# A graph network kernel: x loaded in five pieces with its statistics ahead of the edge keys, and the weight bounds' column sums made by VectorE

## The reference

```
xn = layernorm(x)
gnn: three times  h = x @ W; agg = sum over edges of h[src] * dinv[src] * dinv[dst] + h * dinv^2 + b
     x = layernorm(relu(agg)) * g + beta           (widths 1024, 512, 256)
mix: z = logmap0(proj(xn));  h = z @ w_qkv;  batchnorm over the nodes, relu
     s = depthwise and grouped 1x1 of h;  linear attention of [h, s];  w_res;  projections onto the ball
x = x + gnn + mix
ffn: of layernorm(x) the rows with the 1561 greatest router weights go through gelu(x @ w1 + b1) @ w2 + b2
out = x + ffn's part
```

## Time and profile before

| what | value |
|---|---|
| three runs | 1561.70, 1556.98, 1564.74 us, median 1561.7 |
| the profiled execution | 1556.77 us, span 1554.9 us |
| TensorE busy | 1381.6 us, 89% of the span |
| VectorE, ScalarE, GpSimd busy | 56%, 35%, 35% |
| chain of waits, by engine | PE 67%, DVE 24%, issue 4%, DMA 2%, ACT 2%, POOL 1% |
| GpSimd's scatters | 416, 436.8 us busy and 127.9 between them, the first at 81.75 us |
| load of the flag into a register | three steps on VectorE's queue at L637, 16.8 to 17.7 us |

### The profile page before, as it was taken

One profiled execution on the slowest core, in us unless ns is written; L12 is line 12 of the kernel. 1 busy time (PEld: TensorE's weight loads), 2 busy tenths in 40 slices (PEclk: granted clock), 3 DMA queues, 4 the chain that ended last, 5 costly groups with the idle time before them and its releaser, 6 DMA issues.

```text
span 1554.9 us, 20788 instructions
## 1 busy us (share of the span) xinstructions
PE 1381.6 (89%) x7353; PEld 948.3 (61%) x7353; DVE 867.7 (56%) x1519; ACT 538.1 (35%) x952; POOL 545.6 (35%) x537
## 2 busy tenths in 40 slices
PE   0998997987973899999999999999999899958995
PEld 0576765655752566666666666666666555646775
DVE  6674167758669255555555322222222598778766
ACT  1315062423421344444444323222222122337962
POOL 1078777777777777500000000000000852023100
PEclk9997699998986999999999999999999999989998
DMA  9940000000022222221222032222222344310002
GB/s 292 299 145 1 1 1 1 1 1 1 1 57 55 67 61 59 71 69 51 68 70 60 21 115 61 61 60 60 60 60 60 101 121 133 89 41 1 1 1 83
DMA packets 46076, 99.53 MB, mean 64 GB/s; under 512 B 18962, under 2 KB 31135, under 8 KB 45885
## 3 DMA queue, kind: packets, MB, share of 16 engines
q1 hardware_dynamic: 32698, 98.55, 22.3%
q0 software_dynamic: 13312, 0.13, 0.6%
HBM read 75.79 MB, written 22.85 MB: 63 GB/s over the span
## 4 chain that ended last, share of the span: by engine, by line
PE 67%; DVE 24%; issue 4%; DMA 2%; ACT 2%; POOL 1%; DVEq 0%; SPq 0%; ACTq 0%; POOLq 0%
PE psum L1506 63%; DVE scr L877 5%; DVE scr L1100 4%; PE psum L1797 1%; DVE scr L1058 1%; DMA rows<-in_x 1%; POOL acc L529 1%; DVE scr L879 1%; DVE scr L1051 1%; DVE scr L875 1%; DVE big L1035 1%; DVE scr L1062 1%; DVE scr L1048 1%; DVE scr L1045 1%; DVE scr L882 1%
## 5 line engine op out<-in xcount | busy, mean ns | idle before, releaser
L508 POOL DMA_INDIRECT counts<-big,eidx x416 | 436.8, 1050 | 200.8 <-issue 127.9
L1506 PE MATMUL psum<-rows,scr 125*125 125x512 f16 x1250 | 278.3, 381 | 11.6 <-DVE scr L1048 9.4
L1506 PE MATMUL psum<-big,scr 125*125 125x512 f16 x1250 | 278.5, 379 | 1.0 <-DVE big L952 1.0
L1506 PEld LDWEIGHTS psum<-rows,scr 125*125 125x125 f16 x1250 | 170.2, 137 | 113.6 <-DVE scr L1048 10.1
L1506 PEld LDWEIGHTS psum<-big,scr 125*125 125x125 f16 x1250 | 169.7, 136 | 95.4 <-DVE big L952 1.5
L524 POOL MEMSET big<- 128x4 f16 x1 | 0.1, 115 | 557.0 <-PE psum L1506 557.0
L1506 PE MATMUL psum<-wb,scr 128*125 128x512 f16 x600 | 133.7, 379 | 0.0
L1506 PEld LDWEIGHTS psum<-wb,scr 128*125 128x125 f16 x600 | 81.7, 136 | 47.8 <-ACT scr L1358 0.3
L924 DVE TENSOR_SCALAR scr<-psum,col 125x256 f32<-125x256 f32 x25 | 12.1, 484 | 172.0 <-PE psum L1506 172.0
L1506 PE MATMUL psum<-wb,big 128*125 128x256 f16 x600 | 76.2, 281 | 23.7 <-DVE big L1111 21.1
L1506 PE MATMUL psum<-big,wm 128*128 128x313 f32 x312 | 91.3, 436 | 2.4 <-issue 2.4
(11 more groups left out here) (346 smaller groups left out, 2087.2 us busy)
## 6 DMA issues: line engine op xcount, KB each, us to landing
scr<-counts SPq DMA_DIRECT2D x75, 683.6 KB
counts<-wb SPq DMA_DIRECT2D x25, 683.6 KB
counts<-big,eidx POOLq DMA_INDIRECT x416
scr<-counts SPq DMA_DIRECT2D x75, 79.3 KB
scr<-in_x SPq DMA_DIRECT2D x25, 125.0 KB
rows<-in_x SPq DMA_DIRECT2D x1, 2800.0 KB
out<-acc SPq DMA_DIRECT2D x5, 560.0 KB
wb<-in_w SPq DMA_DIRECT2D x1, 2048.0 KB, 10.9
```

The source lines that it names most:

```text
L508: pool.indirect_dma_start(cells, bass.IndirectOffsetOnAxis(ap=eidx[:, r * EQ + g:r * EQ + g + 1], axis=0), evalue[:, at_c:at_c + 1], None, ...
L1506: return pe.matmul(o, l, r, start=start, stop=stop)
```

## The change

- x is loaded in five pieces of five tiles, each with its own semaphore, and the clears are issued only when the last has landed. VectorE takes the statistics of a piece when it is there.
- On VectorE the keys, the flag and its load into a register come behind z's scale.
- ScalarE loads the table of the square root before it waits for the variance.
- On TensorE the flag's sum, the Gram rows, the rounds, the turnings and the degree products are put in another order.
- The bounds: VectorE sums the columns of `ssw`, `ssg`, `ssb` and `ss1` into seven columns (`sums7`), and TensorE adds these over the partitions with one call in place of 40.

In the diff, the moved block of keys and flag is shown once, where it is added; `sums7` is seven new columns in `col`.

```diff
@@ -75,9 +75,9 @@
     "bounds_read", "n4root_done", "tanh_done", "fnorm_done",
 )
 DVE_MILESTONES = (
-    "flag_part", "flag_ready", "xvar_done", "ratio2_done", "ratio_done", "zscale_ready",
+    "xvar_done", "ratio2_done", "ratio_done", "zscale_ready", "flag_part", "flag_ready",
     "index_ready", "value_ready", "edges_ready", "reach_ready", "needed_ready", "needs_ready",
-    "nzrow_done", "gram_copied", "dinv_read", "wp_done", "bnvar_done", "bn_done", "be2w_read",
+    "nzrow_done", "gram_copied", "dinv_read", "squares_summed", "wp_done", "bnvar_done", "bn_done", "be2w_read",
     "n4_ready", "f4_ready", "fscale_done", "router_done", "negw_done", "least_done", "last_done",
     "bound_found",
 )
...
@@ -358,9 +359,12 @@
         dst_w = bass.AP(a["dst_pad"].tensor, PADE - HALO, [[EC, ER], [1, EW]])
         load(edst_i, dst_w, "edges_loaded")
         load(esrc_i, src_w, "edges_loaded")
-        load_rows(x_rows, a["x"].rearrange("(t p) d -> p t d", p=P), "x_loaded")
+        x_tiles = a["x"].rearrange("(t p) d -> p t d", p=P)
+        for c in range(NC):
+            load_rows(x_rows[:, c * G:(c + 1) * G, :], x_tiles[:, c * G:(c + 1) * G, :], f"x{c}_loaded")
 
         sp.wait_ge(sem("zi_ready"), 2)
+        sp.wait_ge(sem(f"x{NC - 1}_loaded"), ROWS_IN)
         for t in range(T):
             load_rows(counts_dram[t], zi[:, (T - 1 - t) * P:(T - 1 - t) * P + N], "counts_cleared")
         load(wq, a["wq"].rearrange("(k p) n -> p k n", p=128), "mixw_loaded")
@@ -613,31 +617,9 @@
             done.settle()
 
 
-        dve.wait_ge(sem("edges_loaded"), 32)
-        edge_keys(dve, done, ekey, esrc, edp, edt, wkey)
...
-        dve.wait_ge(sem("x_loaded"), ROWS_IN)
         for t in range(T):
+            if t % G == 0:
+                dve.wait_ge(sem(f"x{t // G}_loaded"), ROWS_IN)
             done.did(dve.bn_stats(stats[:, t, :], x_rows[:, t, :]))
         done.settle()
         for t in range(T):
@@ -690,6 +672,29 @@
         done.settle()
         dve.scalar_tensor_tensor(out=z_shift, in0=means, scalar=-1.0, in1=z_scale, op0=ALU.mult,
                                  op1=ALU.mult).then_inc(milestone("zscale_ready"), 1)
+
+        dve.wait_ge(sem("edges_loaded"), 32)
+        edge_keys(dve, done, ekey, esrc, edp, edt, wkey)
+        dstf = wkey
+        done.did(dve.tensor_copy(dstf, edst_i))
+        done.settle()
+        mid, nxt, far_ = (free(dstf, HALO + s, [[1, EC]]) for s in (0, 1, HALO))
+        done.did(dve.tensor_tensor(fwd, mid, nxt, ALU.is_gt))
+        done.did(dve.tensor_tensor(bwd, mid, far_, ALU.is_equal))
+        done.settle()
+        done.did(dve.scalar_tensor_tensor(out=bwd, in0=mid, scalar=float(N), in1=bwd, op0=ALU.is_lt, op1=ALU.mult))
+        done.settle()
+        done.did(dve.tensor_tensor(fwd, fwd, bwd, ALU.max))
+        done.settle()
+        dve.tensor_reduce(flagf[:ER], fwd, AX, ALU.max).then_inc(milestone("flag_part"), 1)
+        dve.wait_ge(sem("flag_sum"), 1)
+        done.did(dve.tensor_scalar(flagf[0:1], bank(7, 1, 1), 1.0, None, ALU.min))
+        done.settle()
+        dve.tensor_copy(flagi[0:1, 0:1], flagf[0:1]).then_inc(milestone("flag_ready"), 1)
+
+
+        dve.wait_ge(milestone("flag_ready"), AFTER["flag_ready"])
+        far = dve.value_load(flagi[0:1, 0:1], min_val=0, max_val=1)
 
         done.settle()
         for r in range(ROUNDS_EQ):
@@ -778,6 +783,11 @@
             done.did(dve.tensor_tensor(gw[:, k, 0:512], bank(4 + 2 * k, 128, 512), wq[:, k, 0:512], ALU.mult))
             last = dve.tensor_tensor(gw[:, k, 512:768], bank(5, 128, 256, 256 * k), wq[:, k, 512:768], ALU.mult)
             last.then_inc(sem("wgw_done"), 1)
+        dve.wait_ge(sem("squares_done"), 2)
+        for n, (part, lo, hi) in enumerate(((ssw, 0, 8), (ssg, 0, 8), (ssb, 0, 8), (ssw, 8, 12), (ssg, 8, 12),
+                                            (ssb, 8, 12), (ss1, 0, 4))):
+            last = dve.tensor_reduce(sums7[:, n:n + 1], part[:, lo:hi], AX, ALU.add)
+        last.then_inc(milestone("squares_summed"), 1)
         for m in range(NT):
             last = dve.tensor_scalar(wp[:, m, :], wp[:, m, :], wdw[:, m:m + 1], None, ALU.mult)
         last.then_inc(milestone("wp_done"), 1)
@@ -1195,6 +1205,7 @@
 
         act.wait_ge(sem("ident_ready"), 1)
         act.copy(ident16[:, :], ident[:, :]).then_inc(milestone("ident16_ready"), 1)
+        act.preload_act_table(ACT.Sqrt)
         act.wait_ge(sem("eps_ready"), 2)
         act.wait_ge(milestone("xvar_done"), AFTER["xvar_done"])
         act.activation(rstd, ca, ACT.Sqrt).then_inc(milestone("xroot_done"), 1)
@@ -1506,8 +1517,6 @@
             return pe.matmul(o, l, r, start=start, stop=stop)
 
         pe.wait_ge(sem("ident_ready"), 3)
-        pe.wait_ge(milestone("flag_part"), AFTER["flag_part"])
-        mm(bank(7, 1, 1), ones[:ER, 0:1], flagf[:ER], True, True).then_inc(sem("flag_sum"), 1)
 
         pe.wait_ge(milestone("ident16_ready"), AFTER["ident16_ready"])
 
@@ -1565,31 +1574,33 @@
             return last
 
         turn_z(0)
-        gram_rows(0, 2)
+        gram_rows(0, 3)
+        pe.wait_ge(milestone("flag_part"), AFTER["flag_part"])
+        mm(bank(7, 1, 1), ones[:ER, 0:1], flagf[:ER], True, True).then_inc(sem("flag_sum"), 1)
+        gram_rows(3, 6)
         count_alike(0)
+        gram_rows(6, 7)
         count_alike(1)
-        gram_rows(2, 4)
+        gram_rows(7, 8)
         count_alike(2)
-        gram_rows(4, 5)
+        turn_z(1)
         count_alike(3)
-        turn_z(1)
-        gram_rows(5, 10)
+        gram_rows(8, 12)
+        turn_z(2)
         turn_edges("index", 2, bwd)
         turn_edges("value", 3, fwd)
-        turn_z(2)
-        gram_rows(10, 11)
+        gram_rows(12, 13)
         turn_reach()
-        gram_rows(11, 12)
+        gram_rows(13, 14)
         turn_needed()
-        for b in range(T - 12):
-            last = gram_rows(12 + b, 13 + b)
-            if b < T - 13:
-                degree(b)
+        for b in range(T - 14):
+            degree(b)
+            last = gram_rows(14 + b, 15 + b)
             if b == 3 or b == 7:
                 turn_z(3 if b == 3 else 4)
         last.then_inc(sem("zsum_done"), 1)
-        degree(T - 13)
-        degree(T - 12)
+        for b in range(T - 14, EC // EB - 2):
+            degree(b)
 
         pe.wait_ge(milestone("nzrow_done"), AFTER["nzrow_done"])
         for m in range(2):
@@ -1597,7 +1608,7 @@
         for k in range(2):
             last = mm(bank(1, 128, 1, 416 + k), zrow[:, k * 128:(k + 1) * 128], ones[0:1, 0:1], True, True)
         last.then_inc(sem("gram_done"), 1)
-        for b in range(T - 11, EC // EB):
+        for b in range(EC // EB - 2, EC // EB):
             degree(b)
 
         pe.wait_ge(milestone("gram_copied"), AFTER["gram_copied"])
@@ -1626,16 +1637,8 @@
             last = mm(bank(5, P, D2), free(be1c[:, k:k + 1], 0, [[0, P]]), w2[:, k, :], k == 0, k == 7)
         last.then_inc(sem("be2w_done"), 1)
 
-        pe.wait_ge(sem("squares_done"), 2)
-        for k in range(4):
-            mm(bank(6, 128, 1, 22), ones[:, :], ss1[:, k:k + 1], k == 0, k == 3)
-        n = 0
-        for L, nk in ((0, 8), (1, 4)):
-            for s in (ssw, ssg, ssb):
-                for k in range(nk):
-                    last = mm(bank(6, 128, 1, 16 + n), ones[:, :], s[:, 8 * L + k:8 * L + k + 1], k == 0, k == nk - 1)
-                n += 1
-        last.then_inc(sem("bounds_done"), 1)
+        pe.wait_ge(milestone("squares_summed"), AFTER["squares_summed"])
+        mm(bank(6, 128, 7, 16), ones[:, :], sums7, True, True).then_inc(sem("bounds_done"), 1)
 
 
         pe.wait_ge(milestone("bn_done"), AFTER["bn_done"])
```

More of the change, by code:

```diff
@@ L150, in _build @@
     kones = sb("kones", [128, 128], F32)
-    col = sb("col", [128, 888], F32)
+    col = sb("col", [128, 895], F32)
     at = {"scr": 0, "col": 0, "wm": 0, "big": 0}
@@ L307, in _build @@
     reach = d2in[:ER]
+    sums7 = c_(7)
     xpoly, z_scale, z_shift = wv, y_scale, y_back
```

## The result

| | before | changed |
|---|---|---|
| median of 11 executions each | 1561.7 us | 1551.9 us |
| lowest, highest | 1555.8, 1593.9 | 1543.1, 1553.9 |
| profiled execution, span | 1556.8, 1554.9 | 1553.65, 1551.8 |

The ratio is 0.9929 (0.9907 to 0.9951), a gain of 0.7%. By the medians that is 9.8 us, about half of the 19.1 forecast; the time, 1552, lies inside the range and 11 above the forecast. The two profiled executions are only 3.1 us apart.

The account below looks back on a forecast made before the run. Chain 67% TensorE, 24% VectorE; bounds 14.3, clock 2.5 and front 2.3 sum to 19.1 us off the profiled 1556.8 (1537.7); with the executions' mean of 1560.0 as base, 1541, range 1531 to 1554.

Parts of the forecast that it names:

- Bounds by VectorE: Bounds, 175.24 to 189.85: one seven-column call replaces 40 on TensorE, gaining 14.3 us; VectorE's seven reductions cost nothing.
- The clock behind it: Hidden layer's first 24 matmuls, behind the bounds: upper clock level, 6.4 us instead of 8.87, another 2.5 us.
- rival 1: Hidden layer still starts at the lower clock because of the wait for the roots; 1543 to 1544 us, chance 0.17.
- x at 17.3: Start of the kernel: without clears, x lands whole at 17.3 us in place of 20.28.
- Rival 2: Pieces of x each pay their own delay, x lands at 31; 1554 to 1555 us, chance 0.08.
- Keys and flag 11.5, comparisons at 38.4: VectorE behind z's scale at 26.9: keys, flag and register load take 11.5 us, so comparisons start at 38.4.
- Rounds that each take 4.53: TensorE's four rounds behind the comparisons: ready from 44.3, 4.53 us each, the fourth ending at about 66.9.
- In the one-hot stage TensorE does a block and a Gram row in 3.50 us: One-hot stage from 79.8: this pace puts ScalarE's squares at 113.3 and TensorE's restart at 135.1; front gains 2.3.
- Clears behind x: Clears and scatters end about 2 us later; covered, since w2 is there 14 us before it is wanted.
- rival 3: Slower than before: late clears delay w2, holding ScalarE's squares, TensorE and VectorE; 1568 us with 40 us late, chance 0.03.
- Rival 4: The shortened stretch doesn't shorten the program, another wait ends at the same time; 0 to 7 off, 1557, chance 0.04.
- The base: Whole kernel: the four executions' mean, 1560.0 us, from which the gain is taken, not the profiled 1556.8.

Follow-up runs that it names:

- e8: Changed kernel without the clears' wait for x; measured once, 2015.6 us, on a chip where the kernel before took 2040.6.
- e1: Changed kernel with the Gram row ahead of each degree product again, as before; median 1546.9 us, ratio 0.989.
- e3: Changed kernel with the 40 one-column sums back on TensorE and no reductions; 1562.9 us, ratio 1.0009.
- e9: Changed kernel with fifteen wide matmuls in TensorE's wait for the first one-hot block; median 1541.6 us, ratio 0.989.
- e10: Kernel before with the bounds' part and seven wide matmuls in TensorE's wait for the first one-hot block; median 1541.2 us, ratio 0.989.
- e2: Kernel before with the bounds' part alone (seven reductions, one matmul); 1548.9 us, ratio 0.9897.
- e4: Kernel before with each degree product ahead of its Gram row in the one-hot stage; 1562.8 us, ratio 1.0018.
- e11: Kernel before with bounds' part, x in pieces, clears behind x, early table load, keys ahead of statistics, seven wide matmuls in the wait; 1537.9 us, ratio 0.9868.

## Why the prediction was half right

- **Bounds by VectorE**: right. One call of 0.28 us, TensorE 15.5 us shorter to the hidden layer (14.3 forecast; the product with wb ahead takes 8.63 us, 1.2 less than before, at a higher clock), all seven reductions 0.54 us and hidden.
- **The clock behind it**: right, 8.87 to 6.57 us; rival 1 is out. ScalarE's chain did not take it back.
- **x at 17.3**: wrong, 19.11. The step "without clears, 3.69 MB at that rate" took 250 GB/s for x alone and got 215; by e8 x's time doesn't depend on the clears. This cost 1.8 us, with landings from 18.33 to 19.41 in the five profiles with this front (the changed kernel, e1, e3, e8, e9). Rival 2's delays of 3.4 us a piece did not come: the statistics of the five pieces start at 8.4, 11.4, 14.3, 16.9 and 19.1.
- **Keys and flag 11.5, comparisons at 38.4**: 12.6 and 41.26. The mis-sized term is the register load, "1.0": the load itself took 1757 ns where it took 553 before, and VectorE idled 2.17 us. With x's 1.8 this makes the comparisons 2.9 us late.
- **Rounds that each take 4.53**: the first took 6.21 (the line at 47.23 above). TensorE has done its Gram rows and waits 3.75 us for the comparison, and the granted clock is 0.50 from 48 to 51. So the fourth round ended 29.3 us behind the start of the comparisons, not 28.5. All five profiles with this front have this fall, also e9, and none of the others. From there to the one-hots were 12.0 us, not 12.9, so these start at 82.57, 2.8 late, and the front's gain of 2.8 there was nothing. The 12.9 isn't a fixed length: VectorE's idle time behind the branch on the flag, ahead of L733, is 4.48 us here and 3.57 to 6.13 in the five profiles, and the one-hots start between 80.89 and 83.78. No run tells why.
- **"In the one-hot stage TensorE does a block and a Gram row in 3.50 us"**: the step that failed. It is 6.36 in the profiled execution; from the one-hots to the squares are 46.1 us, not 33.5. These 12.6 and the 2.8 make the restart late by 15.1 (150.20 against 135.1, less 0.3 in ScalarE's part). With the wait filled (e9) the row of before holds again.
- **Clears behind x**: right that they cost nothing, rival 3 is out; but they are issued 4.8 us later than before (80.7, 75.9), not 2, the first scatter starts at 86.83 (81.75) and w2 is issued at 94.57 (89.89). ScalarE's squares at 128.66 follow TensorE's last turning of z without waiting for w2, so this is covered. Nothing is gained by it either (e8).
- **Rival 4**: out, but the lead shrinks a little behind it, where I counted each microsecond in full: L871 is 5.0 us earlier, the accumulation of the mixing (L917, before L907) starts 4.3 us earlier (266.5, 270.8) and its last instructions 3.3 (513.9, 517.2), the span is 3.1 shorter. The mean clock in 210 to 515 is 0.88, before 0.89; that this takes the 1.7 us there was not tested.
- **The base**: I took the mean of four executions, 1560.0, but all durations from one in which the clock hadn't fallen. A gain read in that execution is right only for executions like it: 1543.1 is 12.6 below before's lowest, e9's median 15.2 below before's, and in the changed kernel eight of 11 executions lie above the lowest group. That 1552 lies within the range is partly luck: the range was widened for rivals 1 and 2, which did not come, and a fall of the clock in the one-hot stage was no rival.

So of the 19.1 us the bounds gave some 15 to 17. The front gave nothing that these runs can tell from none, even with the wait filled: e9 is 1.2 us ahead of e10 at L871, but 0.8 of these are VectorE's idle time behind the branch (3.57 and 4.38), and the medians differ by 0.4 the other way. Without filling its best executions are some 3 us slower. The fall of the clock took the rest; this last part is what is left over and was not measured by itself.

The Trainium skill (TensorE: Matmul & The Clock Gate, Part 1: The HAM clock gate) says that the cost of warming up is run-variable for the same kernel, because the monitor runs freely beside the program. e2 beside before agrees in kind: the same instructions up to 140 us, 8 us apart. The page puts the penalty of that ramp at under 1% of a typical kernel span. e2's 8 us are 0.5%, but a fall in the middle of a kernel can cost more: e4's 42 us are 2.7% of 1557.

## What to carry to other kernels

Before working from one profiled execution, see to which group of executions it belongs, and look for waits of TensorE ahead of thin matmuls: there the next change may pay for a clock that this profile doesn't show falling. In this kernel wide matmuls into an unused bank were a cheap cover for such a wait; in e11 they did not keep the clock up in the two blocks at 128 us. When a transfer is cut into pieces, leave the work that doesn't need it beside the transfer and put only the rest behind it.

## What the runs showed of the hardware

- The granted clock fell to 0.50 and stayed there for 27 us (86 to 113, the changed kernel) or 82 (86 to 168, e4) while TensorE was busy without a gap from the first block on, with matmuls of 25, 256, 125 and 1 columns. The same mix ran at 1.00 in the kernel before. In the first round of comparisons, with 512 columns, it was back after some 3 us (48 to 51).
- It fell without any idle time of TensorE inside rows of thin products alone: at 128 in e11 (25 columns), at 178 in the kernel before (1 column).
- The same register load took 553 ns before, 545 to 556 in all profiles with the keys first, and behind z's scale 1757, 1912, 1737, 1543 and 758 ns in the changed kernel, e1, e9, e8 and e3. No run tells why.
- x in ten transfers moves at 215 GB/s alone, and its landing is the same within the spread of 1.1 us when clears bring the total to 262.
